# Attention scores and masks by TensorE, leaky ReLU by ScalarE, filler products, and GpSimd's pieces in halves, in a four-mixer graph network kernel

## The reference, cut to what matters

```python
def _L1_gnn_ref(h, adj_matrix, W, a):
    Wh = jnp.einsum('bnf,fo->bno', h, W)
    s1 = Wh @ a1
    s2 = Wh @ a2
    e = s1[:, :, None] + s2[:, None, :]
    e = jnp.where(e >= 0, e, ALPHA * e)
    e = jnp.where(adj_matrix[None] == 0, -jnp.inf, e)
    attention = jax.nn.softmax(e, axis=-1)
    return jnp.einsum('bij,bjo->bio', attention, Wh)
...
def _L2_gnn_ref(x, adj_mask, Wqkv, Wo):
    scores = jnp.einsum('btd,bsd->bts', q, k) * scale + adj_mask
    scores = jnp.where(causal, scores, NEG)
    attn = jax.nn.softmax(scores, axis=-1)
    return jnp.einsum('bts,bsd->btd', attn, v) @ Wo
...
_, U = jnp.linalg.eigh(L_norm)
```

## Time and profile before

| | |
|---|---|
| median of 3 runs | 1161.13 us (1157.04 to 1161.92) |
| profiled execution | 1159.08 us, its span 1157.4 us |
| busy share of the span | PE 76%, PEld 53%, DVE 72%, ACT 41%, POOL 19% |
| mean granted PE clock | 0.851 |
| first GAT section | from 654.25 us |
| GpSimd's recurrence for the eigenvectors | 984.84 to 1073.05 us |

### The profile page before, as it was taken

The page is one execution under the profiler, slowest core; times in us unless marked ns, Lnnn a source line. Parts: engine busy times, 40 slices in busy tenths (PEclk is TensorE's granted clock), DMA queues, the critical chain, the costliest instruction groups (busy, mean ns, idle before and its releaser), DMA issues.

```text
span 1157.4 us, 14411 instructions
## 1 busy us (share of the span) xinstructions
PE 878.6 (76%) x4032; PEld 613.0 (53%) x4038; DVE 832.3 (72%) x3265; ACT 476.3 (41%) x1047; POOL 224.8 (19%) x716
## 2 busy tenths in 40 slices
PE   4699989999999999999996457665275165665398
PEld 3588854555557666655556345444253044454265
DVE  6867778877777888777769766764867887556633
ACT  0058755544333444434340133342134155565275
POOL 2111111111111111111110110100211211888000
PEclk9999999999999999999996555555555588999599
DMA  7000000000000000000000000000000000000022
GB/s 246 1 1 1 1 1 1 1 1 1 0 1 1 1 1 1 2 0 1 1 1 1 0 1 1 1 0 1 0 0 1 0 1 1 1 1 1 0 73 73
DMA packets 13974, 12.21 MB, mean 11 GB/s; under 512 B 1091, under 2 KB 10822, under 8 KB 13894
## 3 DMA queue, kind: packets, MB, share of 16 engines
q1 hardware_dynamic: 10704, 8.46, 2.2%
q10 hardware_dynamic: 3190, 2.84, 0.7%
HBM read 7.10 MB, written 4.19 MB: 10 GB/s over the span
## 4 chain that ended last, share of the span: by engine, by line
issue 44%; PE 18%; DVE 16%; POOL 15%; ACT 6%; POOLq 0%; DVEq 0%; ACTq 0%
PE bank L495 16%; POOL col_root L322 7%; POOL t L354 2%; ACT T L398 2%; DVE X L711 2%; POOL PP L354 2%; DVE HT L710 2%; ACT T L459 2%; POOL u L354 2%; PE bank L505 2%; DVE stat L718 1%; POOL XI L326 1%; DVE tt L710 1%; DVE m L1039 1%; ACT sg L478 1%
## 5 line engine op out<-in xcount | busy, mean ns | idle before, releaser
L442 ACT ACTIVATE G<-bank,bias 128x512 f32<-128x512 f32 (+1 forms) x252 | 159.8, 635 | 248.7 <-PE bank L495 247.8
L495 PE MATMUL bank<-HT,wih 128*128 128x512 f32 (+1 forms) x504 | 248.3, 579 | 0.5 <-ACT HT L428 0.5
L402 ACT COPY T<-bank 128x512 f32<-128x512 f32 x144 | 83.6, 581 | 259.5 <-PE bank L495 226.3
L322 POOL TENSOR_TENSOR col_root<-sa,neg_half 128x1 f32<-128x1 f32 x126 | 79.3, 629 | 491.4 <-DVE sa L712 491.4
L495 PE MATMUL bank<-H,whh 128*128 128x512 f32 (+1 forms) x288 | 135.7, 553 | 0.0
L398 ACT ACTIVATE T<-X,nbias,rstd 128x128 f32<-128x128 f32 x256 | 104.3, 485 | 18.6 <-DVE nbias L711 18.6
L505 PE MATMUL bank<-ident,T 128*128 128x128 f32 x256 | 57.0, 363 | 54.3 <-ACT T L459 30.2
L495 PEld LDWEIGHTS bank<-HT,wih 128*128 128x128 f32 x504 | 80.1, 193 | 10.1 <-issue 3.8
L495 PEld LDWEIGHTS bank<-ST 128*128 128x128 f32 x254 | 47.8, 203 | 71.2 <-DVE ST L710 43.4
L505 PEld LDWEIGHTS bank<-ident,T 128*128 128x128 f32 x256 | 37.7, 182 | 86.2 <-ACT T L459 50.8
L711 DVE SCALAR_TENSOR_TENSOR X<-bank,sm,X 128x128 f32<-128x128 f32 x128 | 36.0, 344 | 54.7 <-PE bank L495 54.3
(11 more groups left out here) (324 smaller groups left out, 1895.1 us busy)
## 6 DMA issues: line engine op xcount, KB each, us to landing
out_x<-T SPq DMA_DIRECT2D x16, 256.0 KB, 2.3
wih<-in_WihT ACTq DMA_DIRECT2D x1, 1024.0 KB
whh<-in_WhhT ACTq DMA_DIRECT2D x1, 1024.0 KB
qkvT<-in_WqkvT ACTq DMA_DIRECT2D x1, 192.0 KB
wg<-in_Wg ACTq DMA_DIRECT2D x2, 64.0 KB
l3w<-in_L3W ACTq DMA_DIRECT2D x2, 64.0 KB
adjT<-in_adjT ACTq DMA_DIRECT2D x1, 64.0 KB
adj<-in_adj SPq DMA_DIRECT2D x1, 64.0 KB, 1.9
```

What stands on the lines that cost most here:

```text
L322: e.tensor_tensor(out=col["root"][:, :], in0=sa[:, 0:1], in1=neg_half[:, :], op=ALU.pow).then_inc(root_ready, 1)
L402: e.copy(out=dst[:, :], in_=src[:, :]).then_inc(done, 1)
L442: e.activation(G[x.h][:, gate, 0:n], gate_bank(k)[:, 0:n], ACT.Tanh if gate == 2 else ACT.Sigmoid, bias=bias[:, 4 * (x.p - 1) + gate:4 * ( ...
L495: mm = lambda out, l, r, start=True, stop=True: e.matmul(out, l, r, start=start, stop=stop)
```

## The change

- The GAT scores are accumulated by PE in one bank: the mask (a product of `ident` with `gmask`), the second score vector, and the first score vector as four products with a broadcast right side. ACT applies the leaky ReLU (`Prelu`) out of PSUM; DVE keeps only the reduction.
- The causal scores likewise: the mask is a product of `ident` with `cmask`, the factor is folded into `mqk`, exp and DVE's reduction read PSUM. ACT instead of DVE copies the values `H`.
- `keep_clock(2)` puts two bf16 products of a constant, 128 x 512, into bank 6, up to three times in a slot. The histogram moves to bank 7.
- GpSimd's tables and products are cut in halves. They start on `lull`, a semaphore that DVE raises just before it turns to an attention half: tables of the next block at a block's first two stops, products of the block before at its third and fourth. The signs are placed accordingly.

```diff
+def lulls():
+
+
+    blocks, h, m = [], 0, 0
+    for ps in range(len(POINTS)):
+        for b in range(NB):
+            block = []
+            for s in range(KB):
+                if (b * KB + s) % PACE[ps] == PACE[ps] - 1:
+                    if s < KB - 1:
+                        m += 1
+                        block.append((m, h))
+                    h += 1
+            blocks.append(block)
+        h += 2
+    return blocks
+
+
+LULLS = lulls()
+
+
+def products(n):
+
+    return n // NB * (2 * NB + 2) + (2 * (n % NB + 1) if n % NB < NB - 1 else 2 * NB + 2)
...
-    reach = block_ends()[n] + (0 if n % NB == NB - 1 else 2)
+    reach = block_ends()[n] if n % NB == NB - 1 else LULLS[n + 1][3][1]
...
+            HB = KB // 2
             for ps, f in enumerate(POINTS):
-                def table(b):
+                def table(b, j):
                     n = ps * NB + b
-                    if b == 0:
-                        e.wait_ge(m_ready, ps + 1)
-                    if n >= 2:
-                        e.wait_ge(p_done, n - 1)
-                    e.tensor_tensor(out=v4(DL[n % 2], KB, f), in0=M[:, 0:f].unsqueeze(1).unsqueeze(1).to_broadcast([P, KB, 2, f]),
-                                    in1=d2[:, ds(b * KB, KB), :].unsqueeze(3).to_broadcast([P, KB, 2, f]), op=ALU.subtract).then_inc(dl_ready, 1)
-                table(0)
+                    e.tensor_tensor(out=v4(DL[n % 2], KB, f)[:, ds(j * HB, HB)], in0=M[:, 0:f].unsqueeze(1).unsqueeze(1).to_broadcast([P, HB, 2, f]),
+                                    in1=d2[:, ds(b * KB + j * HB, HB), :].unsqueeze(3).to_broadcast([P, HB, 2, f]), op=ALU.subtract).then_inc(dl_ready, 1)
+
+                def product(b, j):
+                    pb = v4(PB[(ps * NB + b) % 2], KB + 2, f)
+                    rows = HB if b < NB - 1 or j == 0 else HB - 1
+                    e.tensor_tensor(out=v4(prod, KB, f)[:, ds(j * HB, rows)], in0=pb[:, ds(j * HB + 1, rows)], in1=pb[:, ds(j * HB + 2, rows)],
+                                    op=ALU.mult).then_inc(pr_ready, 1)
+
+                e.wait_ge(m_ready, ps + 1)
+                if ps:
+                    e.wait_ge(p_done, ps * NB - 1)
+                for j in range(2):
+                    table(0, j)
                 for b in range(NB):
+                    n = ps * NB + b
                     if b < NB - 1:
-                        table(b + 1)
-                    n = ps * NB + b
-                    e.wait_ge(p_done, n + 1)
-                    if n:
-                        e.wait_ge(sgn_ready, n)
-                    pb = v4(PB[n % 2], KB + 2, f)
-                    pr = v4(prod, KB, f)
-                    if b < NB - 1:
-                        e.tensor_tensor(out=pr, in0=pb[:, 1:KB + 1], in1=pb[:, 2:KB + 2], op=ALU.mult).then_inc(pr_ready, 1)
-                    else:
-                        e.tensor_tensor(out=pr[:, 0:KB - 1], in0=pb[:, 1:KB], in1=pb[:, 2:KB + 1], op=ALU.mult).then_inc(pr_ready, 1)
-                        e.tensor_tensor(out=pr[:, KB - 1, 0], in0=pb[:, KB, 0], in1=pb[:, KB + 1, 0], op=ALU.mult).then_inc(pr_ready, 1)
+                        if n:
+                            e.wait_ge(p_done, n)
+                        for j in range(2):
+                            e.wait_ge(lull, LULLS[n][j][0])
+                            table(b + 1, j)
+                    if b:
+                        if n >= 2:
+                            e.wait_ge(sgn_ready, n - 1)
+                        for j in range(2):
+                            e.wait_ge(lull, LULLS[n][2 + j][0])
+                            product(b - 1, j)
+                n = ps * NB + NB - 1
+                e.wait_ge(p_done, n + 1)
+                e.wait_ge(sgn_ready, n)
+                for j in range(2):
+                    product(NB - 1, j)
+                pb = v4(PB[n % 2], KB + 2, f)
+                e.tensor_tensor(out=v4(prod, KB, f)[:, KB - 1, 0], in0=pb[:, KB, 0], in1=pb[:, KB + 1, 0], op=ALU.mult).then_inc(pr_ready, 1)
...
+                        scores = T[g % 2][3] if kind == "gat" else bank[3 * (g % 2) + 2]
                         e.wait_ge(ms, g + 1)
                         for b in range(GB):
-                            i = e.activation(T[g % 2][4][:, ds(b * P, P)], T[g % 2][3][:, ds(b * P, P)], ACT.Exp,
+                            i = e.activation(T[g % 2][4][:, ds(b * P, P)], scores[:, ds(b * P, P)], ACT.Exp,
...
+                        if kind == "gat":
+                            e.wait_ge(g_s, nx + 1)
+                            e.activation(T[nx % 2][3][:, :], bank[3 * (nx % 2) + 2][:, :], ACT.Prelu, alpha=ALPHA).then_inc(g_leaky, 1)
+                        else:
+                            e.wait_ge(q_v, nx + 1)
+                            copy(H[nx % 2], bank[3 * (nx % 2)], q_vs)
...
-                    e.wait_ge(pr_ready, ps * (NB + 2) + (b + 1 if b < NB - 1 else NB + 2))
+                    e.wait_ge(pr_ready, products(n))
...
+            def keep_clock(n):
+
+                for _i in range(n):
+                    mm(half4(bank[6]), identb[:, :], identb[:, :].unsqueeze(1).to_broadcast([P, GB, P]))
...
+                        keep_clock(2)
                         e.wait_ge(es, g + 1)
                         turn(bk[2], t[4]).then_inc(PTs, 1)
                     if nx < NG:
                         e.wait_ge(hs, nx + 1)
                         turn(bk[0], t[0]).then_inc(Ts, 1)
                     if 0 <= g < NG:
+                        keep_clock(2)
                         e.wait_ge(pTs, g + 1)
                         e.wait_ge(whs, g + 1)
                         each(bk[1], part(t[5]), part(t[2] if kind == "gat" else H[g % 2])).then_inc(os_, 1)
+                    keep_clock(2)
                     if nx < NG and kind == "gat":
                         e.wait_ge(g_hT, nx + 1)
                         if nx >= 2:
                             e.wait_ge(g_x, nx - 1)
-                        each(bk[1], part(t[1]), whole(w1))
+                        each(bk[1], part(t[1]), whole(w1)).then_inc(g_w, 1)
+                        mm(half4(bk[2]), ident[:, :], gmask[:, :].unsqueeze(1).to_broadcast([P, GB, P]), stop=False)
+                        mm(bk[2][:, :], bc(wa[:, 1:2]), t[1][:, :], start=False, stop=False)
                         for b in range(GB):
-                            mm(bk[0][:, b:b + 1], t[1][:, ds(b * P, P)], wa[:, 0:1])
-                        mm(bk[2][:, :], bc(wa[:, 1:2]), t[1][:, :]).then_inc(g_w, 1)
+                            i = mm(bk[2][:, ds(b * P, P)], t[1][:, ds(b * P, P)], bc(wa[:, 0:1]), start=False, stop=b == GB - 1)
+                        i.then_inc(g_s, 1)
...
-                        each(bk[2], part(t[2]), part(t[1])).then_inc(q_s, 1)
+                        mm(half4(bk[2]), ident[:, :], cmask[:, :].unsqueeze(1).to_broadcast([P, GB, P]), stop=False)
+                        for b in range(GB):
+                            i = mm(bk[2][:, ds(b * P, P)], t[2][:, ds(b * P, P)], t[1][:, ds(b * P, P)], start=False, stop=b == GB - 1)
+                        i.then_inc(q_s, 1)
...
-                e.tensor_copy(out=mqk[:, :], in_=bank[4][:, 0:P]).then_inc(pre_sb, 1)
+                TS(mqk[:, :], bank[4][:, 0:P], float(D) ** -0.5, None, ALU.mult).then_inc(pre_sb, 1)
...
-                t, bk, m = T[g % 2], bank[3 * (g % 2):], sm[g % 2]
-                e.wait_ge(g_w, g + 1)
-                net(e.tensor_copy(out=m[:, 0:GB], in_=bk[0][:, 0:GB]))
-                for b in range(GB):
-                    i = STT(t[3][:, ds(b * P, P)], bk[2][:, ds(b * P, P)], m[:, b:b + 1], gmask[:, :], ALU.add, ALU.add)
-                net(i)
-                net(STT(t[3][:, :], t[3][:, :], ALPHA, t[3][:, :], ALU.mult, ALU.max))
-                e.tensor_reduce(out=m[:, 4:8], in_=half4(t[3]), axis=AX.X, op=ALU.max, negate=True).then_inc(g_m, 1)
+
+                e.wait_ge(g_leaky, g + 1)
+                e.tensor_reduce(out=sm[g % 2][:, 4:8], in_=half4(T[g % 2][3]), axis=AX.X, op=ALU.max, negate=True).then_inc(g_m, 1)
 
             def att_scores(g):
-                t, bk, m = T[g % 2], bank[3 * (g % 2):], sm[g % 2]
-                e.wait_ge(q_v, g + 1)
-                e.tensor_copy(out=H[g % 2][:, :], in_=bk[0][:, :]).then_inc(q_vs, 1)
                 e.wait_ge(q_s, g + 1)
-                net(STT(half4(t[3]), half4(bk[2]), float(D) ** -0.5, cmask[:, :].unsqueeze(1).to_broadcast([P, GB, P]), ALU.mult, ALU.add))
-                e.tensor_reduce(out=m[:, 4:8], in_=half4(t[3]), axis=AX.X, op=ALU.max, negate=True).then_inc(q_m, 1)
+                e.tensor_reduce(out=sm[g % 2][:, 4:8], in_=half4(bank[3 * (g % 2) + 2]), axis=AX.X, op=ALU.max, negate=True).then_inc(q_m, 1)
...
-                    e.wait_ge(dl_ready, n + 1)
                     for s in range(KB):
+                        if s % (KB // 2) == 0:
+                            e.wait_ge(dl_ready, 2 * n + 1 + s // (KB // 2))
                         k = rec.note(TT(t, pb[:, s + 1], dl[:, s], ALU.mult))
```

(23 more changed lines are left out.)

1 line of the change is left out of this document (removed).

## The result

The changed kernel takes 1141.88 us (median), the kernel before in the same comparison 1161.53: ratio 0.9845, interval 0.9825 to 0.9865. One of its four executions was slow (1191.78 us, granted clock 0.81); the other three took 1140.84 to 1142.85, and the ratio is that of fast runs alone. The profiled execution took 1140.84 us, 18.2 less than that of before, where the prediction had 4.7 less. The direction was right, and the gain nearly four times what I had put down.

A forecast was written before the change was run, and what follows sets the result against it. It took the half-clock attention's chain of waits, 13.42 us per slot, then GpSimd's 88.2 us recurrence as the bound. 1159.08 - 17.9 up to GpSimd's start + 13.2 in the tail gave 1154.4, taken as 1154 us; range 1135 to 1178.

The forecast's parts named there:

- first two groups: First 9.5 us of the attention stage: longer PE section and added leaky ReLU, +1.5 us.
- nine slots: Stretch 663.76 to 785.13: nine slots of 11.65, table load, signs, two stands, cold restart; 117.3 against 121.4, -4.1 us.
- end of pass one: End of the first pass: -1.5 for DVE's scores, +0.85 for filler at half clock, -0.7 us together.
- histogram: Histogram and start of pass two, to 836.71: -3.5 for the table, -1.0 for section and scores, -4.5 us.
- block end, 18.02 us before: Stretch 863.55 to 881.57: 18.02 becomes 12.0 us with DVE no longer blocked, -6.0 us.
- to GpSimd's start: Stretch 881.57 to 978.95: savings on blocked DVE operations against a longer first slot of the second attention, net -1.3 us.
- tail: After GpSimd's recurrence starts: slots grow from 7.87 to 9.26, attention becomes the bound, 101.4 against 88.2, +13.2 us.
- The plain slot: First-attention (GAT) slot: 11.65 us, between 11.05 at full and 16.2 at half clock, falling in two slots of five.
- The signs: Blocks 1 and 2: ACT stands before the sign until GpSimd's product half is done, 3.5 us each.
- The clock holds: Rival: full clock throughout the GAT slots, 11.05 instead of 11.65 us each, 1144 us; chance 0.20.
- Pieces still block: Rival: GpSimd's halved pieces still hold up X's additions and statistics, or DVE's steps come early, 1168 us; chance 0.15.
- The clock doesn't come back: Rival: GAT slots run 16.2 instead of 11.65 us; 1181 us at six slots, 1209 at all twelve; chance 0.15.

The follow-up runs named there:

- e2: The kernel before with the six filler products per slot as the only edit: 1145.21 us, ratio 0.9883.
- e1: The changed kernel without its six filler products per slot: 1151.74 us, ratio 0.9923 to the kernel before.
- F: The filler part of the change, keep_clock(2) in three places; put alone into the kernel before: 1145.21 us, ratio 0.9883.
- S: The part of the change that reworks the scores; put alone into the kernel before: 1157.48 us, ratio 0.9984.
- P: The part with GpSimd's pieces in halves and their signs; put alone into the kernel before: 1158.05 us, ratio 0.9973.
- e3: The kernel before with only GpSimd's pieces halved, put beside DVE's stops, and the signs placed accordingly: 1158.05 us, ratio 0.9973.
- e8: The changed kernel with the copy of H in the second attention back on DVE: 1129.53 us, ratio 0.9744.
- e7: The changed kernel with the signs of blocks 1 and 2 one slot later: 1131.45 us, ratio 0.9758.
- SF: The changed kernel with the whole GpSimd pieces and sign places of the kernel before: 1153.12 us, ratio 0.9931.
- SFP: The changed kernel itself, with score rework, filler and halved pieces together: 1141.88 us, ratio 0.9845.
- e6: The kernel before with filler and halved pieces, and the signs of blocks 1 and 2 one slot later: 1118.05 us, ratio 0.9637.

## Why the prediction was right or wrong, by its steps

| step | forecast | measured |
|---|---|---|
| start of the first section | 0 | -1.1 |
| first two groups | +1.5 | -1.4 |
| nine slots | -4.1 | -2.4 |
| end of pass one | -0.7 | -3.6 |
| histogram | -4.5 | -6.6 |
| two slots | -2.8 | -2.6 |
| block end, 18.02 us before | -6.0 | -5.8 |
| to GpSimd's start | -1.3 | -4.1 |
| tail | +13.2 | +9.4 |
| profiled execution | -4.7 | -18.2 |

The start of the first section is not part of the change; in the traces here it lies anywhere from 653.0 to 656.6.

**The failed step** is the sum's clock outside the plain slots: "+1.5" for the first two groups with a "section longer", "+0.85 for the filler at half clock" at the end of pass one, and only -1.0 of section and scores at the histogram. I had taken the half clock of the kernel before as given there, because PE waits long in these stretches, and reckoned with the filler only as a cost. The rows of before are these two and the 0.50 from 806.19 on in the earlier trace rows:

```profile
654.25:663.76 9.51, 6.61 (x23) 4.64 (x23) 9.10 (x27) 2.71 (x6) 3.77 (x2) 0.50 0.00 0
785.13:806.19 21.06, 10.43 (x37) 7.29 (x37) 10.26 (x36) 5.77 (x16) 2.41 (x2) 0.50 0.01 1
```

The rows after say 0.90, 0.80 and 0.71. What I allowed in these three was -3.7, what came -11.6: 7.9 of the 13.5 us that I was off. The filler alone (e2) does much of it, 7.7 us less in the three together:

```profile
654.10:661.76 7.66, 5.44 (x25) 3.82 (x24) 7.31 (x22) 2.72 (x6) 3.77 (x2) 0.72 0.00 0
774.14:791.93 17.79, 8.19 (x42) 5.23 (x43) 10.25 (x36) 5.78 (x16) 2.42 (x2) 0.71 0.00 0
791.93:819.87 27.94, 8.96 (x42) 6.75 (x43) 24.48 (x37) 4.84 (x15) 7.24 (x2) 0.69 0.00 1
```

But it is not the only part that can. Take the filler out of the changed kernel (e1), and only the first stretch gets longer:

```profile
653.63:663.89 10.26, 7.37 (x24) 4.76 (x24) 7.57 (x29) 3.30 (x7) 4.10 (x4) 0.67 0.00 0
793.24:810.86 17.62, 8.39 (x38) 5.78 (x39) 8.19 (x30) 6.37 (x17) 2.61 (x3) 0.81 0.00 0
810.86:834.76 23.90, 7.90 (x39) 6.37 (x39) 19.06 (x31) 5.42 (x16) 5.19 (x3) 0.75 0.00 0
```

So the first two groups owe their 2 us to the filler (1.4 to 2.2 in all four pairs of kernels that differ by F alone). In the other two stretches S or F lifts the clock, and where one is there with P, the other adds little: against P alone (21.0 and 27.1 us, clock 0.50) S takes 3.4 and 3.2 off, F 3.0 and 2.6, both together 3.5 and 3.2. For S a part of this can be DVE's score work, which is gone there too.

**To GpSimd's start.** -4.1 instead of -1.3. Up to the first product with `mqk` it was 10.9 less where I had 7.5. Followed along the two chains of waits, the blocked block end gave its -7.3 as forecast, and the sign ahead of the first norm -1.9 (-2.1 forecast). The +1.9 for statistics beside pieces came as +3.3: the statistics kept their 0.87, but two subtractions of the norm took 1.86 and 1.94 instead of 0.27 and 0.23. The rest, -5.0, lies in the slot ahead, up to X, where I had put nothing. In the chain of before the sign of block 4 and PE's sums stand on the way there, and in that of the changed kernel exp has that place:

```profile
887.54 1.92 ACT sg L478
...
889.91 1.48 PE bank L495 x3
```

```profile
862.39 1.54 ACT T L501 x8
```

The section fell from 5.47 to 3.75 and the output products from 2.09 to 1.17 in the same slot. With P alone (e3) the whole way up to `mqk` is 9.2 shorter, so most of it is the pieces and their signs.

**The tail.** The mechanism stood: the attention bounds it, through the copy of H; e8 undid that one edit and the tail came back to 88.9. The terms were too large: 0.73 for the copy (e1, 8.60 against 7.87) instead of 0.96, in part since exp closes up behind it (1.41 instead of 1.54), and 0.34 for the filler (e2, 8.21) instead of 0.43. Ten slots of 0.31 are 3.1 of the 3.8 missing.

**What held.** The plain slot, partly by luck: 11.65 forecast, 11.8 the mean of the five plain ones in the stretch. The falls were more frequent than forecast (four in five, not two) and each cost less (0.9 to 1.4, not 1.5), and a slot at the full clock took 10.85, not 11.05. The signs: 3.5 forecast for each stand, 3.62 read, and 7.0 off the nine slots in e7. The table at the start of pass two: -3.5 forecast, 27.3 to 23.9 between SF and SFP. The block end of 18.02: 15.9 in SF, 12.2 with the pieces.

**The rivals.** "The clock holds" gave 1144, near the measured 1142, but by another way: it put 11.05 into the slots, where 11.8 was right. "Pieces still block" fell for X and the statistics, and stands for DVE operations with two inputs in SBUF (1.86 and 1.94 us, above). "The clock doesn't come back" fell: no plain slot got near 16.2, and even without filler (e1) they read 12.4 to 14.6. The Trainium skill's "TensorE: Matmul & The Clock Gate", Part 4, says that transposes don't count as PE-busy in the same way, by which the prediction would have had slots drift towards 16.2. No run here has the turns apart from other products, so none tests that sentence itself.

**Not foreseen** was that the parts aren't additive. P is worth nothing to 3 us alone, 6 to 7 with S, 14 with F, 10 to 11 with both. The traces place the difference in the nine slots. Up to GpSimd's start P takes 14 to 15 us off outside of them (20 with S alone); inside it adds 9.8 alone, 14.7 with S, nothing with F and 2.6 with both. In each case the two slots with the stands grow by 9 to 10 us. It is the other seven that differ: -0.6 alone, +4.6 with S, -9.2 with F, -6.4 with both. So with the filler the halved pieces buy back in seven slots what the stands cost in two, and without it they don't. Why those seven slots get shorter (the clock, or DVE no longer held up) no run separates.

## What to carry to other kernels

Where a chain goes through TensorE once per slot and its clock reads half, first try constant products in the gaps that a wait covers, by themselves and before any rework that justifies itself with the clock: here they gave 13 to 14 us for three lines, and the same work on the way (between turn and output products) added 0.02 to the clock beside them and cost 0.34 us per slot. Run each part of a compound change alone and left out: one part here cost 10 to 11 us inside a change that gained 18 to 20. When an engine's operation moves to another queue, look at what stands behind it there; a copy that was free on DVE cost 8.7 us of the tail on ScalarE (97.6 against 88.9).

## What the runs showed of the hardware

The granted clock answers to products whose results nobody reads: in nine slots it read 0.57 in the kernel before and 0.81 with them as the only edit (e2), and in the kernels with P and later signs 0.61 with the middle pair alone, 0.65 with the first, 0.80 with both outer pairs and 0.96 with four products in each of these. Full or half clock is not a state of the stage but of single stretches: the same section read 2.90 us at 1.00 and 5.47 at 0.50 within one execution of e6. A GpSimd piece beside DVE's additions out of PSUM costs neither anything (1.13 against 1.14 for them, 1.90 in both cases for the piece), and beside an operation with two inputs in SBUF it makes 1.86 us of 0.27.
